# Mixture-of-experts combine weights: spread by DMA through DRAM and applied as the expert activations leave PSUM

## The chip, the cores and the metric

The kernel runs on one core of one Trainium2 chip. The metric is the device time of one execution in microseconds (us). The figure to compare with is the median of three executions of the kernel before, 752.63 us (751.90 to 753.79).

## The reference

The input is `x` (64 sequences, 750 steps, 32 features). Three layers follow each other; `D` is 128, there are 92 patches per sequence, 8 heads and 8 experts:

```python
patches = x[:, idx, :].reshape(B, n_patches, 512)      # patch 16, stride 8 -> 92 patches
h = patches @ W.T + b                                   # (64, 92, 128)

q, k, v = split_heads(layernorm(h) @ w_qkv.T)
attn = softmax(q @ k.T * scale)
attn = einsum('bhij,hg->bgij', attn, reattn_w)          # heads mixed
attn = (attn - mean_heads) * rsqrt(var_heads + 1e-5) * ln_g + ln_b
h = h + (attn @ v) @ w_out.T + b_out

xf = layernorm(h)
scores = softmax(xf @ gate_w.T)
topk_w, topk_i = top_k(scores, 2);  topk_w = topk_w / (topk_w.sum(-1) + 1e-20)
combine[t, topk_i[t]] = topk_w[t]                       # (T, 8), two entries of a row not zero
h1 = relu(xf @ w1[e] + b1[e])                           # for each of the 8 experts
y  = sum_e combine[:, e] * (h1 @ w2[e] + b2[e])
out = h + y + relu(xf @ sw1 + sb1) @ sw2 + sb2          # one shared expert beside the 8
```

## The kernel before, in words

The 64 sequences are worked off in 16 groups of four (`SLOTS` = 4); a group's tile is 128 features by 368 columns (four sequences of 92 patches). All engines run one program of **steps** in the same order, the list `STEPS` (lines 52 to 61), once per iteration `G`. A step is a tuple for one sequence of the attention (`dots`, `max`, `exa`, `exb`, `inv`, `mix`, `sq`, `rstd`, `scale`, `av`, `ev`) or a name for a whole group. `BEHIND` and `LAG` say which sequence or group a step works on in iteration `G`, so that in one iteration the attention of group G runs beside the tokens of group G+1 and the experts of group G-2. Iterations 2 to 13 are a loop on the chip; setup, iterations 0 and 1, and the tail (iterations 14 to 17, with three order lists of their own in `ORDERS_END`) are written out. Each engine executes its own part of the list strictly in that order.

The names that matter here:

- `XE`, `XO`, `TK`, `TH`, `NH`, `TX`: load, transpose, tokens and layernorm of group G+1. `Y0` to `Y7` and `V0` to `V3` make the scores' and the values' operands.
- `OP`, `TH2`, `NH2`, `TX2`: attention output, its layernorm, and the transposed `x2T`, of group G-1.
- `RT`, `R2`, `R3` (function `routing`): the gate's logits and an 18-instruction chain on VectorE that ends in `combine` (line 934), the 8 weights of each token, three copies of them 32 columns apart. Each instruction waits for the one ahead of it.
- `CT`: TensorE transposes `combine` into PSUM, ScalarE and VectorE copy it out as `combT` (lines 653, 771, 1032).
- `Z0` to `Z8`: the first layer of expert e (`Z8` is the shared one), three matmuls each by `products` (lines 335 to 337: high by high, high by low, low by high halves in fp32r). ScalarE empties it with relu and the bias b1 into `act1` (line 786).
- `C0` to `C7`: a matmul of a 0/1 matrix `pick` with `combT` spreads the weights of expert e over the 128 partitions in PSUM (line 660), and VectorE multiplies `act1` with it (line 1041).
- `H0` to `H4`: pairs of experts (`H4` the shared one) are split into a high half (ScalarE, line 753) and a low half (`low_units`, line 405), by GpSimd for `H0`, `H2`, `H4` and by VectorE for `H1`, `H3`.
- `YF`: 27 matmuls of the second layer behind one with `b2_all` that adds the weighted b2 (line 663). VectorE empties it with the residual `h2T` (line 1045). `OT` transposes and stores.

All group steps that use TensorE fill one of three PSUM banks (`ps_fill`, `NBANK` = 3) in turn; `wait_free` makes TensorE wait until the engine that empties the bank's previous content is done, which makes the emptying engine's pace TensorE's affair after two further fills:

```python
FILLS = [step for step in STEPS if isinstance(step, str) and step not in NO_FILL]
BANK = {step: n % NBANK for n, step in enumerate(FILLS)}
```

SP issues two DMAs per iteration: at `XO` the load of `xin` for group G+2, at `OT` the store of `ostage`.

## Time and profile before

| | |
|---|---|
| median of three executions | 752.63 us |
| the profiled execution, its own time | 751.87 us |
| its span, first to last instruction | 750.0 us |
| TensorE (PE) matmuls, busy | 693.2 us, 92% |
| TensorE weight loads (PEld), busy | 627.9 us, 84% |
| VectorE (DVE) | 539.5 us, 72% |
| ScalarE (ACT) | 470.0 us, 63% |
| GpSimd (POOL) | 353.0 us, 47% |
| DMA, mean over the span | 16 GB/s |
| mean granted TensorE clock | 0.97 |

The busy times are those of one profiled execution on the slowest (here the only) core. Matmuls overlap: the busy time of one is longer than the distance to the next, so the pace of TensorE is read from the start times of a timeline or from the pieces of the chain of waits, and not from the mean duration. The chain of waits is followed back from the last instruction, at each step to what released it.

### The profile page before, as it was taken

Reading aid. Unit: us, or ns where it says so; the run is one execution under the profiler, and the core shown is the slowest. Engines: PE = TensorE matmul, PEld = TensorE weight load, DVE = VectorE, ACT = ScalarE, POOL = GpSimd, SP = SyncE. Lnnn points to the kernel's source line nnn. Section 1 sums busy time; section 2 is a strip of 40 time slices with the busy share of each in tenths; the row PEclk is TensorE's granted clock in tenths of the full one; section 3 lists DMA queues with packets and bytes.
Section 4 is the critical chain, followed back from the end, with each engine's and each line's share of the span. In section 5 each row is a group of like instructions: output and inputs, shape, how many; then the busy total and the mean of one; then the engine's idle time right before and its main releaser. Section 6 shows DMA issues by size and latency. Waiting matters only on the chain.

```text
span 750.0 us, 16779 instructions
## 1 busy us (share of the span) xinstructions
PE 693.2 (92%) x5302; PEld 627.9 (84%) x5302; DVE 539.5 (72%) x1559; ACT 470.0 (63%) x1494; POOL 353.0 (47%) x435
## 2 busy tenths in 40 slices
PE   2778999999999999999999999999999999998846
PEld 2568889899898989899898989899898989886735
DVE  1755586968777786968777786968777786966544
ACT  1246476685857666685847666685847676675514
POOL 1534336554553536554554536554554536554302
PEclk9899899999999999999999999999999999998968
DMA  4200000000000000000000000000000000000000
GB/s 99 80 22 1 22 2 22 12 16 8 8 19 10 20 10 20 10 16 8 7 19 10 20 10 20 10 18 7 8 18 10 20 10 2 11 1 11 1 10 11
DMA packets 17058, 12.04 MB, mean 16 GB/s; under 512 B 924, under 2 KB 16776, under 8 KB 17032
## 3 DMA queue, kind: packets, MB, share of 16 engines
q1 hardware_dynamic: 17032, 11.71, 5.7%
q8 instruction: 14, 0.23, 0.1%
q14 instruction: 12, 0.10, 0.0%
HBM read 8.70 MB, written 3.01 MB: 16 GB/s over the span
## 4 chain that ended last, share of the span: by engine, by line
PE 82%; DVE 10%; issue 3%; ACT 2%; DMA 1%; POOL 1%; DVEq 0%; ACTq 0%; POOLq 0%
PE ps_fill L335 16%; PE ps_fill L337 13%; PE ps_fill L336 13%; PE ps_dots L540 11%; PE ps_mix L552 11%; PE ps_fill L495 7%; PE ps_av L560 5%; PE ps_fill L660 3%; DMA xin<-in_x 1%; DVE key L928 1%; DVE top L930 1%; DVE combine L934 1%; DVE yT L798 1%; ACT ex L697 1%; DVE aT L962 1%
## 5 line engine op out<-in xcount | busy, mean ns | idle before, releaser
L1091 POOL TENSOR_TENSOR sum<-sq 92x384 f32<-92x384 f32 x64 | 64.2, 1003 | 203.3 <-ACT sq L705 203.3
L697 ACT ACTIVATE ex<-ps_dots,negmax 128x92 f32<-128x92 f32 x384 | 123.8, 342 | 38.2 <-DVE negmax L943 38.2
L540 PE MATMUL ps_dots<-xT,yT 128*128 128x96 f32 x768 | 96.7, 276 | 7.8 <-ACT ex L697 4.4
L540 PEld LDWEIGHTS ps_dots<-xT,yT 128*128 128x128 f32 x768 | 91.7, 192 | 11.5 <-issue 11.3
L552 PE MATMUL ps_mix<-mixk,probs 128*92 128x128 f32 x768 | 98.5, 280 | 2.1 <-DVE aT L964 1.2
L1085 POOL TENSOR_TENSOR probs<-ex,rinv 128x552 f32<-128x552 f32 x64 | 71.1, 1111 | 52.2 <-DVE rinv L949 52.2
L552 PEld LDWEIGHTS ps_mix<-mixk,probs 128*92 128x92 f32 x768 | 91.0, 165 | 3.4 <-issue 1.6
L1041 DVE TENSOR_TENSOR act<-ps_fill,act 128x368 f32<-128x368 f32 x128 | 64.5, 534 | 40.7 <-PE ps_fill L660 40.3
L786 ACT ACTIVATE act<-ps_fill,vecT 128x368 f32<-128x368 f32 x144 | 76.6, 567 | 27.3 <-PE ps_fill L337 27.1
L405 POOL TENSOR_TENSOR act_split_lo<-act,act_split_hi 128x736 fp32r<-128x736 f32 (+1 forms) x48 | 81.1, 1703 | 25.2 <-ACT act_split_hi L753 24.1
L697 ACT ACTIVATION_READ_ACCUMULATOR ex<-ps_dots,negmax 128x1 f32 x384 | 81.3, 212 | 0.0
L962 DVE TENSOR_TENSOR aT<-ps_mix,arstd 92x360 f32<-92x360 f32 x128 | 61.6, 522 | 5.4 <-ACT arstd L715 4.7
L560 PE MATMUL ps_av<-aT,v_sb 92*64 92x96 f32 x1024 | 57.7, 256 | 3.8 <-DVE aT L964 2.3
L705 ACT ACTIVATE sq<-ps_mix 92x768 f32<-92x768 f32 x64 | 52.3, 817 | 10.8 <-PE ps_mix L552 10.6
L753 ACT ACTIVATE act_split_hi<-act 128x736 fp32r<-128x736 f32 (+1 forms) x80 | 57.1, 753 | 0.9 <-DVE act L1041 0.8
L560 PEld LDWEIGHTS ps_av<-aT,v_sb 92*64 92x64 f32 x1024 | 45.5, 139 | 13.7 <-issue 11.1
L335 PE MATMUL ps_fill<-x2T_hi,w_split_hi 128*128 128x368 f32 x144 | 51.6, 358 | 0.7 <-DVE combT L1035 0.7
L405 DVE TENSOR_TENSOR act_split_lo<-act,act_split_hi 128x736 fp32r<-128x736 f32 x32 | 47.9, 1527 | 5.9 <-ACT act_split_hi L753 5.7
L711 ACT ACTIVATE lnvar<-sumsq,eps 92x96 f32<-92x96 f32 x64 | 24.0, 375 | 41.9 <-POOL sumsq L1098 41.9
L335 PE MATMUL ps_fill<-xT_split_hi,A_hi 128*128 128x368 f32 x128 | 47.7, 372 | 1.9 <-DVE yT L798 1.6
L943 DVE TENSOR_REDUCE negmax<-ps_dots 128x6 f32<-128x552 f32 x64 | 46.3, 723 | 3.3 <-PE ps_dots L540 3.1
L335 PE MATMUL ps_fill<-act_split_hi,w_split_hi 128*128 128x368 f32 x144 | 48.5, 337 | 0.0
(170 smaller groups left out, 1804.1 us busy)
## 6 DMA issues: line engine op xcount, KB each, us to landing
xin<-in_x SPq DMA_DIRECT2D x16, 372.0 KB
out<-ostage SPq DMA_DIRECT2D x16, 184.0 KB
act<-in_L_ffn_w SPq DMA_DIRECT2D x2, 512.0 KB, 4.3
qkv<-in_L_attn_w_qkv SPq DMA_DIRECT2D x1, 768.0 KB, 9.2
ex<-in_L_tok_W SPq DMA_DIRECT2D x1, 256.0 KB
ex<-in_L_attn_w_out SPq DMA_DIRECT2D x1, 256.0 KB
mixw<-in_L_attn_reattn_w SPq DMA_DIRECT2D x8, 0.5 KB
act<-in_L_ffn_sw SPq DMA_DIRECT2D x2, 64.0 KB, 4.4
```

Of the source, the lines that this page charges most:

```text
L335: nc.tensor.matmul(out, s_hi, m_hi, start=start, stop=False)
L336: nc.tensor.matmul(out, s_hi, m_lo, start=False, stop=False)
L337: return nc.tensor.matmul(out, s_lo, m_hi, start=False, stop=stop)
L405: eng.tensor_tensor(lo, act1[:, two, :], hi.bitcast(F32), ALU.subtract).then_inc(done, 1)
L540: last = pe.matmul(ps_dots[:, c // HALF, o:o + NS], yT[:, 2 * s + c // HALF, c % HALF, :, :].rearrange("p h i -> p (h i)"), xT[:, N * s:N ...
L552: last = pe.matmul(ps_mix[0:N, c // HALF, o:o + 128], probs[:, (s - 1) % 2, c, :], mixk[:, :, :].rearrange("p g i -> p (g i)"), start=True ...
L560: last = pe.matmul(ps_av[o:o + DH, NS * (g // 2):NS * (g // 2) + NS], v_sb[:, (s - 2) % SLOTS, DH * g:DH * g + DH], aT[:, s % 2, N * g:N * ...
L697: last = act.activation(ex[:, s % 2, c, :], ps_dots[:, c // HALF, o:o + N], ACT.Exp, bias=negmax[:, c:c + 1], accum_out=sums[:, s % 2, c:c ...
L786: ins = act.activation(act1[:, e, :], ps[:, 0:W], ACT.Relu, bias=vecT[:, e:e + 1])
L962: dve.tensor_tensor(dst, mixed[:, a, :, :, 0:row], scale[:, a, :, 0:row].unsqueeze(2).broadcast_to([N, HALF, HEADS, row]), ALU.mult)
L1041: ins = dve.tensor_tensor(act1[:, e, :], ps[:, 0:W], act1[:, e, :], ALU.mult)
L1085: pool.tensor_tensor(probs[:, s % 2, :, :], ex[:, s % 2, :, :], rinv[:, s % 2, :].unsqueeze(2).broadcast_to([128, CHUNKS, N]), ALU.mult).t ...
```

## The change

- The steps `C0` to `C7`, the matrix `pick` and their matmuls are gone. In place of them SP stores the weights `combine` to a small DRAM tensor at step `R3` (92 x 32 numbers), waits for that, and loads them back with a partition step of 0, so that `spread` holds all 2944 weights of the group in each of the 128 partitions (1472 KB written).
- VectorE empties `Z0` to `Z7` with one instruction, max(x, -b1) times the weight, which is the weighted relu(x + b1) less b1 times the weight. ScalarE keeps only `Z8`. The missing b1 term goes through w2 once, in setup (`pD`), and is added to the rows of b2.
- All five low halves are made by GpSimd.
- `CT` runs one iteration later, since `YF` alone uses `combT` now. A step `hold` on GpSimd copies `h2T` for `YF`, which now runs behind the next group's `OP`.
- `STEPS` and the orders of the tail are new throughout. Three banks remain.

The diff, cut to its core:

```diff
-UNITS_BY_POOL = ("H0", "H2", "H4")
+EXPERTS = tuple(f"Z{e}" for e in range(E))
 UNITS = ("H0", "H1", "H2", "H3", "H4")
...
-    ("dots", 0), "Z0", ("max", 0), "Z1", "Z2", "Z3", "Z4", "C0", ("mix", 0), ("exa", 0), ("sq", 0), "C1", "C2",
+    ("dots", 0), ("max", 0), ("mix", 0), "Z5", "Z6", ("sq", 0), ("av", 0), "Z4", ("exa", 0), "Z3", ("exb", 0),
...
@@ queue of SP
+                if step == "R3":
+                    g = G + LAG[step]
+                    sp.wait_ge(route, N_ROUTE * (g + 1))
+                    sp.dma_start(weights_dram.rearrange("n s e -> n (s e)"), combine[0:N, :, 0:E])\
+                      .then_inc(weights_stored, 16)
+                    sp.wait_ge(weights_stored, 16 * g + 16)
+                    sp.dma_start(spread[:, :, :, :].rearrange("p n s e -> p (n s e)"),
+                                 bass.AP(tensor=weights_dram.tensor, offset=0, ap=[[0, 128], [1, N * SLOTS * E]]))\
+                      .then_inc(weights_spread, 16)
@@ TensorE
+                elif step == "pD":
+                    pe.wait_ge(b1_diag_ready, 1)
+                    pe.wait_ge(experts_loaded, 64)
+                    for e in range(E):
+                        last = pe.matmul(ps[:, 0:128], b1_diag[:, e, :], w2_sb[:, e, :], start=(e == 0),
+                                         stop=(e == E - 1))
-                elif step[0] == "C":
-
-                    pe.matmul(ps[:, 0:W], pick[:, int(step[1]), :], combT[:, :], start=True, stop=True)\
-                      .then_inc(done, 1)
@@ ScalarE
-                elif step[0] == "Z":
-                    e = int(step[1])
...
-                    ins = act.activation(act1[:, e, :], ps[:, 0:W], ACT.Relu, bias=vecT[:, e:e + 1])
+                elif step == f"Z{E}":
+                    at_least(act, units_ready, len(UNITS) * g)
                     wait_filled(act, step, G)
+                    act.activation(act1[:, E, :], ps[:, 0:W], ACT.Relu, bias=vecT[:, E:E + 1])\
+                       .then_inc(emptied[BANK[step]], 1)
@@ VectorE
-                if step[0] == "H" and step not in UNITS_BY_POOL:
-                    low_units(dve, step, G)
-                elif step[0] == "C":
+                elif step in EXPERTS:
+
                     e = int(step[1])
+                    if step == [other for other in order(G) if other in EXPERTS][0]:
+                        dve.wait_ge(weights_spread, 16 * g + 16)
+                        at_least(dve, units_ready, len(UNITS) * g)
                     wait_filled(dve, step, G)
-                    wait_emptied(dve, f"Z{e}", G)
-                    ins = dve.tensor_tensor(act1[:, e, :], ps[:, 0:W], act1[:, e, :], ALU.mult)
-                    ins.then_inc(emptied[BANK[step]], 1)
+                    dve.scalar_tensor_tensor(out=act1[:, e, :].rearrange("p (s n) -> p s n", n=N),
+                                             in0=ps[:, 0:W].rearrange("p (s n) -> p s n", n=N),
+                                             scalar=b1_neg[:, e:e + 1],
+                                             in1=spread[:, :, :, e].rearrange("p n s -> p s n"),
+                                             op0=ALU.max, op1=ALU.mult).then_inc(emptied[BANK[step]], 1)
@@ GpSimd
-                if step in UNITS_BY_POOL:
+                if step in UNITS:
                     low_units(pool, step, G)
+                if step == "hold":
+                    g = G + LAG[step]
+                    wait_emptied(pool, "OP", G)
+                    if present("YF", G):
+                        wait_emptied(pool, "YF", G)
+                    pool.tensor_tensor(still[:, :], ones[:, :], ones[:, :], ALU.mult)
+                    pool.tensor_copy(h2T_held[:, :, :], h2T[:, :, :]).then_inc(held, 1)
```

How the order moves at three places. First VectorE from the instruction that ends `R3` (it writes `combine`) over the end of one iteration (the branch) to the first instructions on the experts in the next, before:

```order
L934 TENSOR_TENSOR combine<-key,top 92x4x3x8
...
L798 COPY v_sb<-ps_fill 92x512
L949 RECIPROCAL rinv<-sums 128x6
L1035 TENSOR_TENSOR combT<-ps_fill,combT 8x368
L982 TENSOR_TENSOR oT_lo<-ps_av,oT_hi 128x4x92
...
L424 COMPARE_AND_BRANCH
L943 TENSOR_REDUCE negmax<-ps_dots 128x6
L1041 TENSOR_TENSOR act<-ps_fill,act 128x368 x3
```

and now (L1090 is the new instruction on the experts, L1098 empties `YF`):

```order
L982 TENSOR_TENSOR combine<-key,top 92x4x3x8
...
L1098 SCALAR_TENSOR_TENSOR fT<-ps_fill,vecT,h2T_held 128x368
...
L1030 TENSOR_TENSOR oT_lo<-ps_av,oT_hi 128x4x92
L1037 TENSOR_REDUCE xsum<-xT 128x4
...
L833 COPY v_sb<-ps_fill 92x512
L1010 TENSOR_TENSOR aT<-ps_mix,arstd 92x3x8x15 x2
...
L453 COMPARE_AND_BRANCH
L991 TENSOR_REDUCE negmax<-ps_dots 128x6
L1090 SCALAR_TENSOR_TENSOR act<-ps_fill,b_neg,spread 128x368 x4
```

`R3` has moved ahead of `YF` and of all eight `Y` steps, and the experts are no longer behind `CT` but behind the DMA.

TensorE at the same turn of the iteration, before (the first row is `CT`, L540 is `dots`, L335 to L337 a `Z`, L660 a `C`, L552 `mix`, L560 `av`):

```order
L495 MATMUL ps_fill<-ident,combine 128x96 x4
...
L424 COMPARE_AND_BRANCH
L540 MATMUL ps_dots<-xT,yT 128x96 x6
L335 MATMUL ps_fill<-x2T_hi,w_split_hi 128x368
...
L660 MATMUL ps_fill<-combT,pick 128x368
L552 MATMUL ps_mix<-mixk,probs 92x128 x6
L660 MATMUL ps_fill<-combT,pick 128x368 x2
L560 MATMUL ps_av<-aT,v_sb 64x96 x8
```

and now (L533 `OT`, L585 `dots`, L597 `mix`, L365 to L367 the first matmuls of `Z5`, L605 `av`):

```order
L533 MATMUL ps_fill<-ident,fT 92x128 x4
...
L453 COMPARE_AND_BRANCH
L585 MATMUL ps_dots<-xT,yT 128x96 x6
L597 MATMUL ps_mix<-mixk,probs 92x128 x6
L365 MATMUL ps_fill<-x2T_hi,w_split_hi 128x368
...
L605 MATMUL ps_av<-aT,v_sb 64x96 x8
```

`Z5` and `Z6` stand ahead of `av`, `Z4` and `Z3` behind it, and nothing at this turn waits for `combine` any more but the DMA's reader.

SP's queue in the loop, before:

```order
L440 DMA xin<-in_x 93x4x256
L480 ISA
L480 DMA out<-ostage 92x4x128
```

and now:

```order
L469 DMA xin<-in_x 93x4x256
L509 REGISTER_ALU
L510 DMA weights<-combine 368x1x8
L512 ISA
L513 DMA spread<-weights 128x2944
L373 ISA
L518 ISA
L518 DMA out<-ostage 92x4x128
```

Two DMAs with a wait between them stand ahead of the output's store.

## Rows read from the trace of the kernel before

**Rows 1.** Busy time in one stretch of the loop, from the table by stretches:
```profile
core 0: us, PE busy (x) PEld busy (x) DVE busy (x) ACT busy (x) POOL busy (x), PEclk, DMA share, GB/s
305.00:350.00 45.00, 44.38 (x353) 40.35 (x353) 35.70 (x105) 30.10 (x97) 23.27 (x30) 1.00 0.05 13
```

**Rows 2.** Timeline of POOL: one step (`shift`) in two iterations that follow each other:
```profile
297.96 0.49 POOL L1123 COPY hT_old<-hT 128x368 f32<-128x368 f32 x1
340.15 0.49 POOL L1123 COPY hT_old<-hT 128x368 f32<-128x368 f32 x1
```

**Rows 3.** Chain of waits near 300 us (start us, us, what): what steps take on TensorE:
```profile
300.81 1.31 PE ps_mix L552 x12
302.12 0.81 PE ps_av L560 x16
302.93 0.40 PE ps_fill L335
303.33 0.23 PE ps_fill L336
...
304.21 1.34 PE ps_dots L540 x12
...
308.26 0.17 PE ps_fill L336
```

**Rows 4.** Groups of instructions by line (busy us, mean ns, idle before and its releaser):
```profile
L660 PE MATMUL ps_fill<-combT,pick 128*128 128x368 f32 x128 | 42.5, 371 | 0.7 <-DVE act L1041 0.3 <-ACT act L786 0.2
L1041 DVE TENSOR_TENSOR act<-ps_fill,act 128x368 f32<-128x368 f32 x128 | 64.5, 534 | 40.7 <-PE ps_fill L660 40.3
L962 DVE TENSOR_TENSOR aT<-ps_mix,arstd 92x360 f32<-92x360 f32 x128 | 61.6, 522 | 5.4 <-ACT arstd L715 4.7
L405 DVE TENSOR_TENSOR act_split_lo<-act,act_split_hi 128x736 fp32r<-128x736 f32 x32 | 47.9, 1527 | 5.9 <-ACT act_split_hi L753 5.7
L1045 DVE SCALAR_TENSOR_TENSOR fT<-ps_fill,vecT,h2T 128x368 f32<-128x368 f32 x16 | 9.6, 600 | 41.3 <-PE ps_fill L337 41.3
L405 POOL TENSOR_TENSOR act_split_lo<-act,act_split_hi 128x736 fp32r<-128x736 f32 x32 | 57.0, 1782 | 25.0 <-ACT act_split_hi L753 23.8
```

**Rows 5.** Timeline of PE where `CT` and the next `dots` start:
```profile
316.14 0.52 PE L495 MATMUL ps_fill<-ident,combine 96*128 96x96 f32 x4 [0.23 <-DVE bias L1030]
316.97 1.57 PE L540 MATMUL ps_dots<-xT,yT 128*128 128x96 f32 x12 [0.31 <-issue]
```

**Rows 6.** Timeline of DVE through `RT`, `R2` and `R3` of one group:
```profile
307.16 0.19 DVE L798 COPY logit<-ps_fill 92x32 f32<-92x32 f32 x1
...
308.48 0.97 DVE L962 TENSOR_TENSOR aT<-ps_mix,arstd 92x360 f32<-92x360 f32 x2
...
310.82 0.18 DVE L911 SCALAR_TENSOR_TENSOR key<-shift_l,rev 92x32 f32<-92x32 f32 x1
...
312.79 0.19 DVE L923 TENSOR_TENSOR hot<-hot 92x32 f32<-92x32 f32 x1
...
313.59 0.17 DVE L927 TENSOR_REDUCE top<-exl 92x4 f32<-92x32 f32 x1
...
315.42 0.32 DVE L934 TENSOR_TENSOR combine<-key,top 92x96 f32<-92x96 f32 x1
```

**Rows 7.** DMA issues (KB each, us to landing), and SP's timeline of the experts' weights:
```profile
qkv<-in_L_attn_w_qkv SPq DMA_DIRECT2D x1, 768.0 KB, 9.2
...
ident<-const_ident SPq DMA_DIRECT2D x1, 64.0 KB, 1.9
...
17.22 0.42 SPq L469 DMA_DIRECT2D act<-in_L_ffn_w  x1
...
18.31 0.43 SPq L471 DMA_DIRECT2D act<-in_L_ffn_w  x1
```

**Rows 8.** The line of the second of these loads, asked alone:
```profile
DMA to landing us min/median/max: 4.8/4.8/4.8
```

**Rows 9.** Timelines of DVE and of SP in the tail, the last group:
```profile
727.65 0.25 DVE L934 TENSOR_TENSOR combine<-key,top 92x96 f32<-92x96 f32 x1
...
745.89 0.26 SPq L480 DMA_DIRECT2D out<-ostage  x1
```

More of the change, by code:

```diff
@@ L136, in order, with first_hidden, last_expert, layout_banks @@
     return STEPS
+def first_hidden(G):
+    return next((step for step in order(G) if step[0] == "Z"), None)
+def last_expert(G):
+    return [step for step in order(G) if step in EXPERTS][-1]
 SETUP = SETUP_START + [step for step in STEPS if present(step, FIRST) and step not in SETUP_START]
 SETUP[SETUP.index("Y5"):SETUP.index("Y5")] = ["pM"]
-SETUP += ["prepE"]
+SETUP += ["pD", "prepE"]
+def layout_banks():
+    last_use = {bank: -1 for bank in range(NBANK)}
+    chosen = {}
+    for n, step in enumerate(SETUP):
+        if step in BANK:
+            last_use[BANK[step]] = n
+        elif step in LAYOUT and not step.startswith("prep"):
+            chosen[step] = min(last_use, key=last_use.get)
+            last_use[chosen[step]] = n
+    return chosen
+BANK.update(layout_banks())
 TAIL = [(step, G) for G in range(END, LAST) for step in order(G) if present(step, G)]
@@ L403, in low_units @@
             hi, lo = [m[:, two, :] for m in act1_split]
[L404 to L405 removed]
+            eng.tensor_tensor(lo, act1[:, two, :], hi.bitcast(F32), ALU.subtract).then_inc(units_ready, 1)
         def bank(step):
@@ L749, in do @@
                     k = int(step[1])
-                    last = f"C{2 * k + 1}" if k < E // 2 else f"Z{E}"
-                    wait_emptied(act, last, G)
+                    for e in range(2 * k, min(2 * k + 2, E + 1)):
+                        wait_emptied(act, f"Z{e}", G)
+                    if step == [other for other in order(G) if other in UNITS][0]:
+                        at_least(act, units_ready, len(UNITS) * g)
+                        if present("YF", G - 1):
+                            wait_filled(act, "YF", G - 1)
                     two = slice(2 * k, min(2 * k + 2, E + 1))
@@ L854, in prepare @@
                 if step == "prepE":
+                    wait_filled(dve, "pD")
                     low = slice((COPIES - 1) * COPY, (COPIES - 1) * COPY + E)
+                    for r in range(COPIES):
+                        rows = slice(COPY * r, COPY * r + E)
+                        last = dve.tensor_tensor(b2_sb[rows, :], bank("pD")[rows, 0:128], b2_sb[rows, :], ALU.add)
+                    last.then_inc(emptied[BANK["pD"]], 1)
+                    wait_emptied(dve, "pD")
                     for r in range(COPIES):
```

92 lines of the change are left out of this document (50 added, 42 removed), and 17 rows, old and new, of tables (ORDERS_END, STEPS).

## The prediction

> **What bounds the kernel now.** I read first the busy time by stretches, since a total mixes setup, loop and tail. In a stretch of the loop TensorE is busy for 44.4 of 45 us, VectorE for 35.7, ScalarE for 30.1 and GpSimd for 23.3, at the full granted clock [rows 1]. So the loop runs at TensorE's pace, and what counts is what TensorE has to do and what newly makes it wait. One iteration takes 42.2 us (340.15 less 297.96) [rows 2]. Then the chain of waits, for the true price of each step on TensorE, since the busy time of one matmul overlaps the next: `mix` 1.31, `av` 0.81, `dots` 1.34, one product of 368 columns 0.17 (so a `Y` or a `Z` 0.51 and `YF` with its 28 some 4.8), and a `V` 0.40 + 2 x 0.23 = 0.86 [rows 3]. Last the timeline around `CT`: TensorE stands for 0.23 us ahead of it and for 0.31 behind it [rows 5], the only waits for routing in the loop.
>
> **The sum is made against the profiled execution's own 751.87 us**, which is 0.8 us under the median of the three runs; that is added at the end.
>
> **C matmuls removed.** Each group loses 8 matmuls of 368 columns. The groups view gives 371 ns for one [rows 4], but that overlaps; the pace is 0.17 us [rows 3], so 8 x 0.17 = 1.36 us per iteration on the engine that bounds. The steps ran in 16 iterations, of which 14 are before the last two of the tail (those go by another sum, below): 14 x 1.36 = **-19.0 us**.
>
> **Gaps at CT.** `CT` now transposes a `combine` that has been ready for half an iteration. The 0.23 and 0.31 us [rows 5] can go, 0.54 us; the lower bound is 0, if TensorE stands there for something else.
>
> **VectorE.** The 8 multiplications of 534 ns become 8 instructions of the kind that empties `YF` (one PSUM operand, one SBUF operand, a pointer scalar), 600 ns [rows 4]: +0.5 us per iteration. The two low halves of 1527 ns go: -3.1. VectorE thus has about 2.5 us less to do, and was not the bound: 0. ScalarE loses 8 emptyings and gets nothing: 0, by TensorE's cover.
>
> **GpSimd** gets two more low halves of 1782 ns [rows 4] and `hold`, a copy like that of `hT_old`, 0.49 us [rows 2], some 4.1 us in all. That takes it from 23.3 of 45 us [rows 1] to about 27, or 61% of a shorter iteration. Behind each low half stand, on GpSimd's queue, the sums for `sq` and the `probs` for `mix` of some sequence. A sequence has a quarter of an iteration, 10 us, for each of its steps, so a delay of 1.8 us is covered; if that cover is gone, `mix` or `av` waits for up to 1.8 us. I take 0. The wait of VectorE's `OP` for `hold` is for a copy made half an iteration earlier: 0.
>
> **A new stall at Y3.** In the new order VectorE has, from the end of `RT` on TensorE to the end of `R3`: 1.3 (307.16 to 308.48), 2.2 (310.82 to 312.98) and 2.15 (313.59 to 315.74) for the three parts of routing, 0.97 for `scale` between them [rows 6], and 0.53 for the low half of `TX`, priced as the 534 ns row [rows 4]. That is 7.2 us. TensorE meanwhile has `TX` (about 0.4 to 0.5, four transposes like `CT` [rows 5]), `YF` 4.8, `mix` 1.3, `Y0` and `Y5` 1.0: 7.5 us. `Y3` then needs the bank of `YF`, which VectorE empties right behind `R3`, 7.2 + 0.6 = 7.8. TensorE waits for about 0.4 us; bounds 0 and 1. With the gaps at `CT` the two come to -0.14 per iteration, over 12 iterations **-1.7 us**.
>
> **The DMA round trip, the step on which all hangs.** The first expert, `Z5`, now waits for `weights_spread`, at the head of VectorE's queue; behind it stand the emptyings of `Z6` and `Z4` and the attention's `ev` and `scale`. How much time is there? `R3` ends 7.2 us after `RT`, TensorE starts `Y3` at 7.8. From there: six `Y` 3.1, `av` 0.8, two `V` 1.7, `OT` 0.4, `dots` 1.3, `mix` 1.3, `Z5` 0.5, together 9.1, so VectorE wants the weights at 16.9. TensorE itself can still fill `Z6`, do `av` and fill `Z4` (1.8 us) before `Z3` needs the bank of `Z5`; with 0.7 for emptying `Z5` that leaves 1.1 us. So the weights have to land by 18.0, which is **10.8 us after R3**.
>
> How long does it take? The store is 368 pieces of 32 bytes. The nearest row is the smallest load, 64 KB in 1.9 us [rows 7]; the other end is the last output store, from its issue at 745.89 [rows 9] to the end of the span, 4.1. I take 1.9, as these are few bytes. The load writes 1472 KB. The experts' weights, 512 + 64 + 512 KB in three loads, were issued from 17.22 on, and the last was issued at 18.31 and landed 4.8 us later [rows 7, 8], 5.9 us for 1088 KB; by their pace 1472 KB take 8.0. The slow end is `qkv`, 768 KB in 9.2 us behind other loads [rows 7], which gives 17.6. I take 8.0, because a row of `spread` is one long run and nothing else is in flight. With 0.2 for two hand-overs the round trip is **10.1 us**, range 9.5 to 21.9, and 0.7 us under what there is. Cost in the loop: 0, with hardly a margin. The Trainium skill (page "DMA: Bandwidth & Descriptors", section on the anatomy of one DMA) fits 2.0 us plus bytes over 436 GB/s for a DMA issued from GpSimd; by it the load would take 5.5 us and the round trip 7.6, well hidden, though no run here shows a broadcast read. The output's store stands behind both DMAs on SP's queue, and has a whole iteration until `ostage` is written again: 0. The load of `xin` is issued at `XO`, behind the first `Z`, so it meets neither.
>
> **Setup.** `pD` adds 8 matmuls with 128 columns in full fp32; six such are a `mix`, 1.31 us, so 1.7. VectorE's part changes by less than a microsecond. TensorE has gaps in setup, so the bounds are 0 and 1.7; I take **+1**.
>
> **Tail.** Here the round trip lies open. Before, from the end of `combine` at 727.90 to the issue of the last store at 745.89, 18.0 us pass [rows 9]. Now: round trip 10.1, `Z0` and `Z1` emptied 1.2, high half 0.8, then four low halves in a row on GpSimd, 7.1 [rows 4], the last six matmuls 1.0, `YF` emptied 0.6, `OT` and its emptying 1.6, in all 22.4, with some hand-overs 23: **+5**. In the iteration before, five low halves on one engine cost some 1 to 2 us more, but `OP` is no longer between `YF` and `TH2` and gives 2.0 back: 0.
>
> **Sum:** -19.0 - 1.7 + 1 + 5 = -14.7, thus 737.2, and 738 against the median. A measurement of this kernel tells about 0.3%, 2.3 us, from no change.
>
> **The rivals.**
>
> *The round trip is longer than its cover (slower).* The place is VectorE's wait at the first `Z` of each iteration. It decides from 10.8 us, and eats the whole gain of 14.7 at 10.8 + 14.7/14 = 11.9 us. For it: 128 partitions and 16 DMA engines read the same 11.8 KB, which no row shows; the store is in small pieces; and the slow end is 21.9. At 14 us each iteration loses 3.2, 14 times 45, and the tail 4 more: 786 us. At 21.9 it would be over 890. Against it: the loads of the experts' weights. Chance 0.22.
>
> *The weights are read slowly from SBUF (no gain).* In the new instruction `spread` is read with a step of 32 numbers, 128 bytes. The nearest row writes `aT` with a step of 15 numbers, and takes 522 ns for 360 elements against 534 for 368 without steps [rows 4], so no penalty shows, but that is a write. If a read took twice the 534 ns, each expert's emptying would take some 1.1 us against 0.5 for the next fill; the Zs come in pairs, and four pairs an iteration with 0.4 us of wait each are 1.6, more than the 1.36 gained: about 754 us. The Trainium skill (page "SBUF — State Buffer", in the section on the DMA port swizzle) says that accesses which cross 16-byte lines pay a penalty, which speaks for this rival. Chance 0.10.
>
> *The new order stalls elsewhere.* A `mix` or `av` that comes 1 us late once per iteration, behind a low half on GpSimd, takes 12 us back: 750. Chance 0.08.
>
> *More than the sum goes.* All small gaps between steps vanish, a further 0.8 us per iteration: 728. Chance 0.06.
>
> *That the change does not do what it says* is out: TensorE's list has no C matmul.
>
> **How the numbers follow.** The forecast, between 730 and 748 by the bounds of the stall at `Y3` (-5 to +7), of setup and of the tail, has 0.54. With the last rival, most of the third, and a part of the DMA rival between 10.8 and 11.9 us, faster by over 0.3% has 0.64; the same 0.08; slower 0.28, from the DMA's 0.20 and parts of the second and third. The range reaches from 724 to 782, where the round trip is 13.7 us; 0.05 is left out below and some 0.15 above.
>
> **What would show it.** Right: the loop's period is near 40.7 us, TensorE stays at 98% of it, the load of `spread` lands within 8 us of its issue, and the first `Z` is emptied without idle time put down to a DMA. The new instruction takes 600 ns; well over 900 would be the second rival. In the tail 23 us from `combine` to the last store's issue. Wrong: VectorE idle ahead of its first expert line, released by a DMA, once per iteration, and TensorE idle 1 us later; or `mix` waiting for GpSimd's `probs`.

## The result, and the profile after

The changed kernel takes **785.71 us** (median of 4, 783.9 to 787.42) against 753.21 for the kernel before in the same comparison (median of 4, 751.9 to 754.99): a ratio of 1.044, 95% interval 1.0409 to 1.0471. It is slower by 32.5 us. 738 was forecast, and the range ended at 782. The profiled execution took 787.42 us, its span is 785.6, its mean granted clock 0.94.

The head of the page, with the slices of the span:

```profile
span 785.6 us, 16622 instructions
## 1 busy us (share of the span) xinstructions
PE 681.7 (87%) x5190; PEld 619.1 (79%) x5190; DVE 541.2 (69%) x1531; ACT 412.9 (53%) x1366; POOL 406.2 (52%) x500
## 2 busy tenths in 40 slices
PE   1687869999999999999999999999999998685735
...
PEclk9679979999999999999999999999999999785967
```

In the middle every slice of TensorE is a 9. What is wrong stands at the ends: in the last six slices it falls to 6, 8, 5, 7, 3, 5, and the granted clock to 7, 8, 5, 9, 6, 7. The time of an execution is best cut where one step recurs. I use the low half of `TX2` on VectorE, once per group (its 3rd start, its 14th, and the end of the span), in these traces:

| kernel | to the 3rd | 11 iterations | period | from the 14th to the end | span |
|---|---|---|---|---|---|
| before | 178.9 | 463.4 | 42.13 | 107.7 | 750.0 |
| after | 187.8 | 455.0 | 41.36 | 142.8 | 785.6 |
| e1_flat_read | 184.0 | 441.3 | 40.12 | 134.8 | 760.1 |
| e2_new_tail | 186.0 | 453.9 | 41.26 | 111.6 | 751.4 |
| e3_new_tail_flat_read | 182.1 | 441.3 | 40.12 | 110.3 | 733.7 |
| e7_no_b1_fold | 179.5 | 452.9 | 41.18 | 112.6 | 745.0 |
| e8_pM_late | 184.5 | 453.3 | 41.21 | 111.2 | 749.0 |
| e9_low_halves_back | 183.8 | 453.6 | 41.24 | 112.0 | 749.4 |
| e11_setup_order | 183.0 | 453.2 | 41.20 | 111.1 | 747.2 |
| e10_all_mended | 179.5 | 439.6 | 39.96 | 112.0 | 731.0 |
| e12_eight_matmuls_more | 178.4 | 451.5 | 41.04 | 114.4 | 744.3 |

The 35.6 us between the spans of before and after are thus +9.0 at the start, **-8.4 in the loop, and +35.1 in the tail**. The first loads do not land at the same time in every execution: VectorE's first instruction starts at 13.6 us before, at 16.1 after, and between 12.9 and 14.7 in the other traces of the table. Differences of 2 us in the first column therefore say little, and 2.5 of the +9.0 may be the loads.

**The loop.** The stretch that stands in [rows 1], now:

```profile
core 0: us, PE busy (x) PEld busy (x) DVE busy (x) ACT busy (x) POOL busy (x), PEclk, DMA share, GB/s
305.00:350.00 45.00, 43.52 (x359) 40.06 (x359) 35.34 (x112) 28.39 (x100) 27.37 (x33) 1.00 0.14 46
```

TensorE is busy for 43.5 of 45 us, where it was 44.4: it waits more than before, not less. GpSimd is at 27.4, as forecast. The gaps at `CT` [rows 5] are gone, and the table of waits from 190 to 600 us has two others, once per iteration each (engine and line, what released it, total us, times, longest):

```profile
PE ps_mix L597 <- DVE aT L1012: 8.8, 10, 1.1
PE ps_dots L585 <- ACT ex L733: 7.1, 10, 0.7
```

The first, 0.88 us, is the stall that the prediction put at `Y3`, one step earlier: `mix` stands right behind `YF`, and needs the `scale` that VectorE does between the parts of routing. The second was not foreseen. ScalarE's timeline shows how it comes about:

```profile
341.45 0.82 ACT L793 ACTIVATE act_split_hi<-act 128x736 fp32r<-128x736 f32 x1 [0.96 <-DVE act L1090]
342.18 0.32 ACT L733 ACTIVATE ex<-ps_dots,negmax 128x92 f32<-128x92 f32 x1
```

The high half `H1` waits for VectorE to empty `Z2`, and behind it in ScalarE's queue stands `exb`, for which TensorE's `dots` waits.

**The instruction and the round trip.** What the trace says of `spread`:

```profile
L1090 DVE SCALAR_TENSOR_TENSOR act<-ps_fill,b_neg,spread x128: 816/867/907, 124.5 to 774.4; 128x368 f32<-128x368 f32 x128
...
  PE ps_fill L367: 21.9, 30
  DMA spread<-weights: 7.7, 2
```

867 ns instead of 600. VectorE waits for the DMA only twice, for 1.0 us at 166 us, in the first iterations of the loop, and for 6.7 us in the last group, where the prediction has the round trip open. From 190 to 600 us it never does. One round trip, first SP's rows, then the first expert of that group on VectorE:

```profile
320.52 0.70 SPq L510 DMA_DIRECT2D weights<-combine  x1
323.33 0.35 SPq L513 DMA_DIRECT2D spread<-weights  x1
```

```profile
330.98 1.64 DVE L1090 SCALAR_TENSOR_TENSOR act<-ps_fill,b_neg,spread 128x368 f32<-128x368 f32 x2 [0.68 <-PE ps_fill L367]
```

The store takes 2.8 us until the load is issued, the load 6.2 (median): 9.1 us from the end of `R3`, landed at 329.5, and the first expert comes at 331.0, released by TensorE and not by the DMA.

**The tail**, cut at the last three starts of the low half of `TX2`. After, then before:

```profile
643.00:704.00 61.00, 49.24 (x325) 44.42 (x324) 31.49 (x83) 25.98 (x86) 27.15 (x34) 0.86 0.09 29
704.00:751.00 47.00, 29.64 (x174) 25.05 (x174) 20.82 (x62) 13.37 (x34) 15.94 (x17) 0.74 0.13 41
751.00:785.00 34.00, 17.58 (x75) 15.55 (x75) 11.87 (x30) 5.54 (x9) 8.06 (x5) 0.70 0.15 50
```

```profile
642.00:682.00 40.00, 39.04 (x307) 34.80 (x305) 29.77 (x84) 27.07 (x90) 20.81 (x27) 1.00 0.02 6
682.00:721.00 39.00, 28.46 (x182) 24.53 (x182) 21.37 (x64) 17.41 (x44) 12.64 (x14) 0.84 0.04 11
721.00:750.00 29.00, 17.58 (x83) 14.90 (x83) 12.43 (x32) 9.69 (x18) 4.88 (x3) 0.74 0.03 7
```

The exact lengths are 60.8, 47.3 and 34.7 us against 40.1, 38.7 and 29.0: +20.7, +8.6, +5.7. The first of them was free of waits before (39 of 40 us busy, full clock). TensorE's largest waits there, with the durations that follow them:

```profile
664.23 1.85 PE L585 MATMUL ps_dots<-xT,yT 128*128 128x96 f32 x12 [1.77 <-ACT ex L733]
671.74 2.52 PE L597 MATMUL ps_mix<-mixk,probs 128*92 128x128 f32 x12 [2.48 <-POOL probs L1139]
...
686.84 0.67 PE L365 MATMUL ps_fill<-oT_hi,woT_split_hi 128*128 128x368 f32 x1 [3.36 <-DVE oT_lo L1030]
```

A `mix` of 1.5 us takes 2.5 here, a matmul of 0.33 us takes 0.67. The granted clock in two of these stretches:

```profile
666.50:668.40 1.90, 1.90 (x9) 1.82 (x9) 0.17 (x1) 1.24 (x3) 0.00 (x0) 0.50 0.00 0
686.80:692.50 5.70, 5.66 (x18) 5.66 (x19) 2.12 (x8) 0.90 (x5) 1.54 (x2) 0.50 0.00 0
```

So behind these pauses TensorE ran at the lower of its two clocks (1.2 GHz), and the pauses cost more than their length. In the first part all waits of TensorE add up to 10.9 us; a mean clock of 0.86 over 61 us is, by an estimate from that row, another 8.5 us. Together they make 19.4 of the 20.7 us.

The second of these waits is the one that the prediction named as a sign of being wrong, `mix` waiting for GpSimd's `probs`. No low half stands in its way:

```profile
670.58 1.11 POOL L1139 TENSOR_TENSOR probs<-ex,rinv 128x552 f32<-128x552 f32 x1 [5.25 <-DVE rinv L997]
```

GpSimd sat idle for 5.25 us until VectorE made `rinv` (step `inv`), which the new order puts behind `CT`, `Z0` and `Z1` in VectorE's queue.

### The profile page after: what moved, and what is told of

It reads as the page before. It is cut to its first block, busy times and chain, and to the rows that moved or that the text cites. A ratio compares the mean times of both kernels' runs of the same rounds, so it can differ in the third digit from the quotient of the medians.

```text
span 785.6 us, 16622 instructions
## 1 busy us (share of the span) xinstructions
PE 681.7 (87%) x5190; PEld 619.1 (79%) x5190; DVE 541.2 (69%) x1531; ACT 412.9 (53%) x1366; POOL 406.2 (52%) x500
## 4 chain that ended last, share of the span: by engine, by line
PE 54%; DVE 24%; issue 7%; ACT 6%; DMA 4%; POOL 3%; SPq 1%; DVEq 0%; ACTq 0%; POOLq 0%
PE ps_fill L365 10%; PE ps_mix L597 9%; PE ps_fill L367 9%; PE ps_fill L366 9%; PE ps_dots L585 8%; DVE act L1090 5%; PE ps_av L605 4%; PE ps_fill L533 4%; DVE aT L1010 3%; ACT ex L733 2%; DMA spread<-weights 2%; DVE hot L960 2%; ACT act_split_hi L793 1%; DVE negmax L991 1%; DMA gate_nat<-in_L_ffn_gate_w 1%
## 5 line engine op out<-in xcount | busy, mean ns | idle before, releaser
L434 POOL TENSOR_TENSOR act_split_lo<-act,act_split_hi 128x736 fp32r<-128x736 f32 (+1 forms) x80 | 127.3, 1600 | 35.9 <-ACT act_split_hi L793 35.7
L1090 DVE SCALAR_TENSOR_TENSOR act<-ps_fill,b_neg,spread 128x368 f32<-128x368 f32 x128 | 107.1, 867 | 29.9 <-PE ps_fill L367 21.9
L597 PE MATMUL ps_mix<-mixk,probs 128*92 128x128 f32 x768 | 102.6, 286 | 25.2 <-DVE aT L1012 21.9
L597 PEld LDWEIGHTS ps_mix<-mixk,probs 128*92 128x92 f32 x768 | 91.3, 168 | 31.4 <-issue 22.7
L585 PE MATMUL ps_dots<-xT,yT 128*128 128x96 f32 x768 | 98.7, 279 | 15.2 <-ACT ex L733 14.5
L585 PEld LDWEIGHTS ps_dots<-xT,yT 128*128 128x128 f32 x768 | 91.5, 193 | 22.1 <-ACT ex L733 12.3
L733 ACT ACTIVATION_READ_ACCUMULATOR ex<-ps_dots,negmax 128x1 f32 x384 | 79.5, 207 | 0.0
L793 ACT ACTIVATE act_split_hi<-act 128x736 fp32r<-128x736 f32 (+1 forms) x80 | 59.1, 765 | 35.5 <-DVE act L1090 35.5
L724 ACT ACTIVATE yT<-ps_fill 128x384 f32<-128x384 f32 x64 | 31.5, 492 | 78.7 <-PE ps_fill L367 78.4
L365 PE MATMUL ps_fill<-x2T_hi,w_split_hi 128*128 128x368 f32 x144 | 56.7, 393 | 11.9 <-DVE act L1090 11.1
L1010 DVE TENSOR_TENSOR aT<-ps_mix,arstd 92x360 f32<-92x360 f32 x128 | 61.6, 522 | 7.8 <-ACT arstd L751 7.7
L605 PE MATMUL ps_av<-aT,v_sb 92*64 92x96 f32 x1024 | 57.8, 256 | 4.4 <-DVE aT L1012 3.5
L605 PEld LDWEIGHTS ps_av<-aT,v_sb 92*64 92x64 f32 x1024 | 46.0, 139 | 13.8 <-issue 10.9
L366 PE MATMUL ps_fill<-x2T_lo,w_split_hi 128*128 128x368 f32 x144 | 50.0, 348 | 0.0
L367 PE MATMUL ps_fill<-x2T_hi,w_split_lo 128*128 128x368 f32 x144 | 50.0, 347 | 0.0
L365 PE MATMUL ps_fill<-xT_split_hi,A_hi 128*128 128x368 f32 x128 | 46.2, 361 | 4.2 <-DVE M L882 1.7
L365 PE MATMUL ps_fill<-act_split_hi,w_split_hi 128*128 128x368 f32 x144 | 48.3, 335 | 0.4 <-POOL act_split_lo L434 0.4
## 6 DMA issues: line engine op xcount, KB each, us to landing
out<-ostage SPq DMA_DIRECT2D x16, 184.0 KB
weights<-combine SPq DMA_DIRECT2D x16, 11.5 KB
```

What stands on the lines that cost most here:

```text
L365: nc.tensor.matmul(out, s_hi, m_hi, start=start, stop=False)
L366: nc.tensor.matmul(out, s_hi, m_lo, start=False, stop=False)
L367: return nc.tensor.matmul(out, s_lo, m_hi, start=False, stop=stop)
L434: eng.tensor_tensor(lo, act1[:, two, :], hi.bitcast(F32), ALU.subtract).then_inc(units_ready, 1)
L585: last = pe.matmul(ps_dots[:, c // HALF, o:o + NS], yT[:, 2 * s + c // HALF, c % HALF, :, :].rearrange("p h i -> p (h i)"), xT[:, N * s:N ...
L597: last = pe.matmul(ps_mix[0:N, c // HALF, o:o + 128], probs[:, (s - 1) % 2, c, :], mixk[:, :, :].rearrange("p g i -> p (g i)"), start=True ...
```

## The experiments

**Theory T** after this reading: the loop does nearly what was forecast; the loss is in the orders that the change writes for the last iterations (`ORDERS_END`), with some in setup. **Rival S**: the slow expert instruction sets everything, in the loop and in the tail. Each experiment was compared with runs of the kernel before on its own chip, whose medians were 752.2 to 752.8 us throughout.

### e1_flat_read: the slow read away

```diff
-    in1=spread[:, :, :, e].rearrange("p n s -> p s n"),
+    in1=spread[:, :, :, :].rearrange("p n s e -> p (n s e)")[:, W * e:W * e + W]
+        .rearrange("p (s n) -> p s n", n=N),
```

> The changed kernel, but VectorE's instruction on expert e reads 368 neighbouring numbers of spread (from 368 e on) in place of every 32nd word; these are the wrong weights, the work and its waits are the same. Theory T (the loss sits in the orders of the last iterations, whose waits are exposed): the instruction falls from 867 to about 600 ns, which gives the loop at most 0.5 us per iteration and the tail some 2 us per iteration, 775 to 781 us. Rival S (the slow read of the weights is the cause): the loop gains another 1 us or more per iteration and the tail comes back too, 755 us or less.

763.56 us (761.91 to 764.65), ratio 1.0145 (1.0093 to 1.0196), 22 us less than after.

```profile
L1090 DVE SCALAR_TENSOR_TENSOR act<-ps_fill,b_neg,spread x128: 554/592/603, 123.0 to 748.9; 128x368 f32<-128x368 f32 x128
```

With neighbouring numbers the same instruction takes 592 ns, what the prediction had priced. The period falls by 1.2 us and `dots` no longer waits for `ex`. The time lies between the two expectations: the slow read is worth 22 us by the medians, more than T gave it and less than all, and the tail is still 27 us longer than before's.

### e2_new_tail: another order for the last iterations

```diff
-ORDERS_END = [[
-    ("dots", 0), ("max", 0), ("mix", 0), ("exa", 0), ("sq", 0), ("exb", 0), ("av", 0), ("rstd", 0), ("dots", 1),
...
+ORDERS_END = [STEPS, [
+    ("mix", 0), "Z8", "CT", ("sq", 0), ("av", 0), "Z0", ("ev", 0), "Z1", ("rstd", 0), ("scale", 0), "Z6", "Z2",
+    ("av", 1), "H4", ("ev", 1), "H0", "OP", "Z3", "TH2", "Z4", "Z5", "NH2", "H1", "Z7", "TX2", "RT", "H2", "R2", "R3",
+    "H3", "YF", "hold", "OT",
+], [
```

> The changed kernel with other orders for two iterations of the tail only: iteration 15 runs the loop's own order (STEPS), iteration 16 puts the Z steps of group 14 under the attention's last chain and under the layernorm of group 15, and YF behind R3. Theory T: iteration 15 falls from 61 to about 41 us and iteration 16 from 47 to about 37, so 30 us less, 755 us. Rival S: the emptying at 867 ns paces these iterations in any order, so less than 10 us are won, over 775 us.

755.58 us (753.24 to 757.74), ratio 1.0046 (1.0019 to 1.0073): **30 us less than after from the order of two iterations alone**, with the instruction still at 866 ns. The three parts of the tail are 39.5, 35.6 and 36.5 us long. The first two have lost 33.0 us, the third is 1.8 us longer.

### e3_new_tail_flat_read: both

> Both edits together (wrong weights again). Theory T: the gain of the new tail plus a few us for the flat read, 745 to 752 us. Rival S: about as e1, since the flat read would already have brought most of it back.

735.75 us (734.95 to 736.27), ratio 0.977 (0.9721 to 0.982). The edits of e1 and e2 add up: -22 and -30 give -50, which is 9 us more than theory T expected here at best. The time is 2 us under the prediction's 738, but by misses that cancel: the period is 40.12 us where the sum has 40.6, the third group still starts 3.2 us later than before, and the tail has an order that the prediction did not price.

### e4_load_twice: a longer round trip

```diff
+    sp.wait_ge(weights_spread, 32 * g + 16)
+    sp.dma_start(spread[:, :, :, :].rearrange("p n s e -> p (n s e)"), ...)
```

> The changed kernel, with the load of spread made twice, the second behind the first's landing; VectorE waits for the second. The round trip grows from about 9.1 to 15.3 us. My step in the prediction (10.8 us of cover from R3 to the first expert): each loop iteration gets 4 to 4.5 us longer, about 45.7 us, and each of the last three iterations some 6: 850 to 860 us. Rival (the cover is larger than worked out): under 2 us per iteration, under 820 us.

877.17 us (873.31 to 883.9), ratio 1.1678 (1.1604 to 1.1753). The period is 47.8 us, 6.4 more, and the time missed the expectation on the high side. The waits from 190 to 600 us, and the granted clock in half an iteration with the wait and in the half behind it:

```profile
DVE act L1094 <- DMA spread<-weights: 45.6, 8, 5.8
PE ps_fill L365 <- DVE act L1094: 31.3, 8, 4.0
```

```profile
305.00:330.00 25.00, 20.44 (x151) 18.68 (x152) 15.47 (x31) 12.87 (x43) 10.99 (x14) 0.86 0.32 120
330.00:353.00 23.00, 22.24 (x176) 20.66 (x176) 17.38 (x64) 12.35 (x42) 14.24 (x19) 1.00 0.12 36
```

A round trip longer by 6.0 us (second load issued at 308.49, the first at 302.47) makes TensorE wait 3.9 us: 2.1 us of cover were unused, so the cover is about 9.1 + 2.1 = 11.2 us, where 10.8 had been worked out. The iteration gets longer by 6.4 us and not by 3.9. The granted clock is lower around the wait: 0.86 over 25 us is, by an estimate, at most 3.5 us more, enough for the rest. Whether the wait also costs something by moving other steps was not measured apart.

This trace also says what does not set the two costly iterations of the tail. Its last three parts take 61.6, 47.3 and 41.3 us, against 60.8, 47.3 and 34.7: with a round trip 6.0 us longer the first grows by 0.8 us, the second not at all, and only the last by 6.7. The expectation of some 6 us for each was wrong, and the DMA is out as the cause of the +20.7 and +8.6.

### e5_step_32_bytes and e6_flat_layout: can the read be made fast?

```diff
-    sp.dma_start(weights_dram.rearrange("n s e -> n (s e)"), combine[0:N, :, 0:E])
+    sp.dma_start(bass.AP(tensor=weights_dram.tensor, offset=0, ap=[[E, N], [N * E, SLOTS], [1, E]]),
+                 combine[0:N, :, 0:E])                                               # e5
+    for s in range(SLOTS):                                                           # e6
+        sp.dma_start(bass.AP(tensor=weights_dram.tensor, offset=N * s, ap=[[1, N], [W, E]]),
+                     combine[0:N, s, 0:E])
```

VectorE's index into `spread` is changed to fit in both.

> The tail's new order stays (755.58 us with the weights read at a step of 128 bytes, 735.75 with neighbouring numbers). The store writes the weights in another order, so that one expert's 368 weights lie 32 bytes apart in each row of spread instead of 128. Theory L (a read at any step over 16 bytes pays the same): the instruction stays at 866 ns, the time at 753 to 758. Theory B (only a large step pays, by banks or lines of 64 bytes or more): the instruction falls to between 600 and 700 ns and the time to 737 to 745. The store is still 368 pieces of 32 bytes, so the round trip should stay at 9.1 us.

> A true layout with one expert's 368 weights side by side: the store is four DMAs (one per sequence) of 736 pieces of 4 bytes each, all else as in e2_new_tail. The instruction must come to 592 ns, as in e1_flat_read. If the store in small pieces is as fast as before (theory: a DMA costs by its fixed part), the round trip stays under 10 us and the time is 736 to 739. If the pieces cost (rival), with 2944 pieces against 368 and four issues in a row, the round trip is 11 to 14 us, over its cover of some 11, VectorE waits for the DMA once per iteration, and the time is 745 to 790.

e5: 754.51 us (752.6 to 757.95), ratio 1.0043 (1.0025 to 1.0061), no different from e2, as theory L has it. e6: 998.7 us (997.16 to 1001.03), ratio 1.3288 (1.3254 to 1.3322), far beyond both expectations. The instruction in e5 and in e6:

```profile
L1082 DVE SCALAR_TENSOR_TENSOR act<-ps_fill,b_neg,spread x128: 831/895/975, 120.6 to 740.9; 128x368 f32<-128x368 f32 x128
```

```profile
L1084 DVE SCALAR_TENSOR_TENSOR act<-ps_fill,b_neg,spread x128: 554/593/602, 134.2 to 984.2; 128x368 f32<-128x368 f32 x128
```

895 ns (median) at a step of 32 bytes, 867 at 128, 593 for neighbours. The Trainium skill (page "SBUF — State Buffer", in the section on the DMA port swizzle) says that accesses which cross 16-byte lines are penalized, without a figure. The three rows agree with it, as both steps are over 16 bytes and pay about the same; a step under 16 bytes was not tried. And e6's stores, one group:

```profile
338.27 9.66 SPq L503 DMA_DIRECT2D weights<-combine  x4
355.67 0.34 SPq L507 DMA_DIRECT2D spread<-weights  x1
```

2944 pieces of 4 bytes in four DMAs take 17.4 us until the load can be issued; 368 pieces of 32 bytes in one took 2.8. Neighbouring numbers alone were worth 20 us (e3 against e2), and e6 is 243 us slower than e2. It has both smaller pieces and four DMAs in place of one; the two were not separated.

### e7, e8 and e11: the setup

e7 leaves out the fold of b1 (seven matmuls of `pD`, the three additions to `b2_sb`). e8 and e11 only move steps:

```diff
-SETUP[SETUP.index("Y5"):SETUP.index("Y5")] = ["pM"]
+SETUP[SETUP.index("BS"):SETUP.index("BS")] = ["pM"]                                  # e8
+SETUP[SETUP.index("BS"):SETUP.index("BS")] = ["pM", "prepX", "pD", "prepE"]          # e11, no others elsewhere
```

> As e2_new_tail, but the fold of b1 into the bias rows is left out (seven of the eight matmuls of pD and the three additions to b2_sb), so the output lacks b1 times w2. Theory: the fold lies on the path of setup ahead of the first row maximum, matmuls about 1.8 us and additions 0.9; the start of the third group comes 2 to 3 us earlier than 185.98 and the time is 752.5 to 754. Rival: it is hidden behind other work in setup; no change, 755 to 756.

> As e2_new_tail, but in setup pM (the product of the weights for the output) comes ahead of BS, its first user, and not ahead of Y5, which in the new order of steps has moved to the front of the Ys. Theory: the Ys of the first group no longer wait for VectorE's copy of M and its matmuls, TensorE idles less between 30 and 45 us and the time falls by 1 to 3 us, to 752.5 to 754.5. Rival: setup is bounded by VectorE and the loads at that place, so that the same wait appears one step later: 755 to 756, no change.

> As e2_new_tail, but in setup pM, prepX, pD and prepE come ahead of BS. e7 without the fold of b1 was 8.5 us faster, and e8 with pM moved 3.6 us. Theory: both costs are costs of place, since VectorE does the additions of prepE and the five instructions of prepX at a moment when TensorE waits for it; at BS VectorE stands idle for 2 us. Then the first hT_old (52.97 in e2, 50.31 in e8, 48.44 in e7) comes at 47 to 49 and the time is 747 to 750. Rival: what setup adds is work that has to be done somewhere ahead of the first maximum: 751 to 752, as e8.

e7: 747.12 us (746.84 to 748.7), ratio 0.994 (0.9919 to 0.9961). e8: 751.92 (750.28 to 753.16), ratio 0.999 (0.9978 to 1.0003). e11: 748.86 (745.46 to 749.39), ratio 0.9939 (0.9915 to 0.9963). VectorE in e2 at the end of setup, ahead of the first row maximum:

```profile
46.73 0.88 DVE L893 TENSOR_TENSOR b_sb<-ps_fill,b_sb 8x128 f32<-8x128 f32 x3 [1.79 <-PE ps_fill L557]
...
48.67 0.73 DVE L983 TENSOR_REDUCE negmax<-ps_dots 128x6 f32<-128x552 f32 x1
```

The same steps in e11:

```profile
40.49 0.88 DVE L892 TENSOR_TENSOR b_sb<-ps_fill,b_sb 8x128 f32<-8x128 f32 x3 [0.24 <-PE ps_fill L556]
...
44.41 0.73 DVE L982 TENSOR_REDUCE negmax<-ps_dots 128x6 f32<-128x552 f32 x1 [1.16 <-PE ps_dots L576]
```

The fold holds VectorE's queue in e2 for 3.7 us (1.79 waiting for `pD`, then 1.9 from 46.73 on), with the first softmax behind it. Moved ahead of `BS` it starts 6.2 us earlier, and the first row maximum (`negmax`) 4.3 us earlier. By the medians e7 is 8.5 us under e2, e8 3.7 and e11 6.7; the third group's start gives 6.5, 1.5 and 3.0. Part of the gap between the two figures is that e2's profiled execution was 2.3 us under its median. e7 and e8 came out below what was expected of them, e11 within it. So leaving the fold out is worth 6.5 to 8.5 us, where the prediction had 1 for all of setup, and moving steps alone wins 3.0 to 6.7 back. How much of that is the fold's is not shown, since e11 moves `pM` and `prepX` with it.

### e9_low_halves_back: H1 and H3 on VectorE again

```diff
+UNITS_BY_POOL = ("H0", "H2", "H4")
+UNITS_BY_DVE = ("H1", "H3")
...
+    done = units_ready if step in UNITS_BY_POOL else dve_units
```

> As e2_new_tail, but the low halves H1 and H3 are on VectorE again, as in the kernel before. If moving them to GpSimd was free in the loop, as the prediction has it, putting them back costs or gives nothing while VectorE keeps up: with the expert instructions at 866 ns VectorE gets 2 x 1.53 us more, 38.4 of 41.3 us, and every emptying and aT behind H1 comes up to 1.5 us later. Theory V (VectorE is already the engine that TensorE waits for, at mix and dots): the period rises from 41.27 by 0.5 to 2 us, 762 to 780. Rival G (the low halves on GpSimd delay probs and thereby the attention): the period falls, 750 to 754.

752.79 us (750.86 to 755.04), ratio 1.0003 (0.9983 to 1.0023); the period is 41.24 us against 41.26. In this loop, which still has the waits at `mix` and `dots`, it does not matter which engine makes them, though VectorE's busy time rises to 38.2 of 45 us. V falls. G's sign does not show in the period either, though the time lies in its range: of the 2.8 us under e2, 2.2 stand in the first column of the table, where the loads differ from one execution to the next. The row that surprised:

```profile
L430 DVE TENSOR_TENSOR act_split_lo<-act,act_split_hi x32: 872/913/1004, 132.5 to 740.6; 128x736 fp32r<-128x736 f32 x32
```

913 ns here, where the same instruction had a mean of 1527 in the kernel before [rows 4].

### e10_all_mended: a version that beats both

The new tail, the setup of e11, and two moves in the loop, one for each of TensorE's waits:

```diff
-    "XO", ("ev", 1), ("mix", 1), "Z7", "Z2", ("exa", 1), ("sq", 1), "OP", "H1", "Z1", ("exb", 1), "shift",
+    "XO", ("ev", 1), ("mix", 1), "Z7", "Z2", ("exa", 1), ("sq", 1), "OP", "Z1", ("exb", 1), "H1", "shift",
...
-    ("inv", 2), "V2", "RT", "R2", ("rstd", 2), "TX", ("scale", 2), "R3", ...
+    ("inv", 2), "V2", "RT", "R2", ("rstd", 2), ("scale", 2), "TX", "R3", ...
```

> As e11_setup_order, with two more moves in the loop's order: H1 goes behind the second exb, and the second-to-last scale ahead of TX. They are meant for the two stalls of TensorE per iteration that are left (0.72 us ahead of dots for ex, 0.76 ahead of mix for aT). Theory: both are set by what stands ahead on ScalarE and VectorE, so the period falls from 41.27 to between 40.1 and 40.7, and the time to 735 to 742, below both kernels. Rival: the wait comes back one step later (YF, Y0 or TK), period 41.0 to 41.3, 746 to 750.

**731.57 us** (729.77 to 734.04), ratio **0.9717** (0.9691 to 0.9743): 21 us faster than the kernel before, 54 faster than after, with 867 ns per expert instruction. It came out better than its expectation. The loop's stretch, and what is left of TensorE's waits in it:

```profile
305.00:350.00 45.00, 44.38 (x353) 40.85 (x353) 37.17 (x109) 27.10 (x93) 25.70 (x33) 1.00 0.15 47
```

```profile
PE ps_mix L588 <- DVE aT L1003: 2.7, 10, 0.3
```

TensorE is back at 44.4 of 45 us, the wait ahead of `dots` is gone, the one ahead of `mix` is 0.27 us. The two moves gave 1.24 us per iteration (41.20 to 39.96), and 17 us against e11.

### e12_eight_matmuls_more: the price of the largest term

```diff
                 elif step == "CT":
+                    for _ in range(E):
+                        pe.matmul(ps[:, 0:W], b2_all[:, :], combT[:, :], start=True, stop=True)
```

> As e10_all_mended, plus eight matmuls of 368 columns ahead of the transposes of CT, in the form of the C matmuls that the change removed; their result is written over. This prices the largest term of the prediction by itself, in a loop that waits for nothing but TensorE. Theory: 0.17 us each on the pace, 1.36 us per group; the period rises from 39.96 to 41.3 us and the time from 731.6 to 750 to 755 (16 groups, 22 us). Rival: part of them goes into time in which TensorE waits anyway (0.3 us ahead of mix), or the price is the 0.33 us that the groups view gives one (2.6 per group, 773 us); below 0.1 us each, under 745, the term was too high.

747.22 us (746.13 to 749.36), ratio 0.994 (0.9917 to 0.9963), 15.6 us over e10. TensorE's timeline at the place, first e10, then e12:

```profile
321.78 1.50 PE L576 MATMUL ps_dots<-xT,yT 128*128 128x96 f32 x12
323.12 0.49 PE L524 MATMUL ps_fill<-ident,combine 96*128 96x96 f32 x4
```

```profile
324.00 1.50 PE L576 MATMUL ps_dots<-xT,yT 128*128 128x96 f32 x12
325.28 1.57 PE L690 MATMUL ps_fill<-combT,b_all 128*128 128x368 f32 x8
326.70 0.49 PE L524 MATMUL ps_fill<-ident,combine 96*128 96x96 f32 x4
```

From `dots` to the transposes it is 1.34 us in the one and 2.70 in the other: 1.36 on the spot, to the hundredth the prediction's term per iteration. The period rises by only 1.08 (39.96 to 41.04), so later steps give 0.28 back; which ones is open. So one such matmul was worth 0.13 to 0.17 us, the time missed its expectation on the low side by 3 us, and the term of -19.0 was too large by about a fifth at most (14 x 1.08 = 15.1).

## Why the prediction was wrong

The sign was wrong, and most of the chance of "slower" lay on a rival that was not the cause. Cut as in the table, the sum had -2 us up to the third group, -16.5 in the 11 iterations and +3.6 in the tail; measured were +9.0, -8.4 and +35.1. By its own steps:

- **C matmuls, -19.0.** Right in kind and nearly in size: e12 prices them at 15 to 19 us over 14 iterations.
- **Gaps at CT, -0.54 per iteration.** Right: no wait for routing is left in the loop. What its going gave was not measured apart.
- **The stall at Y3, +0.4.** The chain through routing, `scale` and `TX` was the right one. The wait was 0.88 us, and it came at `mix`, the first step behind `YF` that needs any of VectorE's work; I had looked only for the next bank. In e10, with `scale` one place forward, 0.27 is left.
- **VectorE's expert instruction, 600 ns, "0".** Mis-sized: 867. The price was taken from a row with the same operands but without a step in the SBUF read. The second rival had the mechanism, a slow read, and I gave it a tenth, because a *write* with a step showed no penalty [rows 4]. The sentence of the Trainium skill that it cites (page "SBUF — State Buffer", in the section on the DMA port swizzle: each access that crosses to a new line pays a penalty) agrees with the rows of e1 and e5. Its place was wrong: TensorE does not wait at the `Z` pairs but at `dots`, by way of `H1` on ScalarE. Its 754 us left out the +6 of setup and tail; by the prediction's own terms it comes to 760. Worth: 22 us by the medians (e1). Between the two profiled executions it is 25.5 us, 13.7 in the loop, 8.0 in the tail and 3.8 ahead of the third group, where VectorE's first instruction also starts 3.0 us earlier.
- **Low halves and hold on GpSimd, 0.** Right in the loop for the low halves (e9); `hold` was not tested by itself.
- **DMA round trip, 10.1 us against 10.8.** 9.1 against about 11.2: right, and the first rival (0.22) is out. Its parts were off in both directions: the store took 2.8 instead of 1.9, the load 6.2 instead of 8.0. The Trainium skill (page "DMA: Bandwidth & Descriptors", section on the anatomy of one DMA) has a fit for a DMA issued from GpSimd, and the estimate of 5.5 us by it was closer than the row I used, though this DMA was issued from SP. That rival's estimate of 786 us happens to be the measured time, for a reason that does not hold; the coincidence says nothing for it.
- **Setup, +1.** Mis-sized: the third group starts 9.0 us late, of which 2.5 may be the loads. The term counted TensorE's matmuls and left out that `prepE` stands ahead of the first maximum in VectorE's queue and waits there for `pD` (e7, e11), and that the new order puts `pM` ahead of seven of the eight `Y`s, where five stood ahead of it before (e8).
- **Tail, +5: the step that failed.** The last group took what was worked out, 23.7 us from `combine` to the last store's issue (757.80 to 781.52) for 23, and +5.7 in all; in part by luck, since the first expert came 8.8 us behind `combine` where the sum has a round trip of 10.1, and the rest took 14.9 for 12.9. But "in the iteration before ... 0" was written for two iterations whose orders are new from the first line to the last. They cost +20.7 and +8.6. I had read the order of the loop step by step and not theirs. e2 shows that the order is the cause: 30 us come back from it alone, with the read still slow; e4 shows that the DMA is not.

The mis-sized terms are thus 29 us (two iterations of the tail), +9.0 for +1 up to the third group, and 22 for the read. They overlap and cannot be added: of the read's share of the tail 6.9 us lie within the 29. e10, with another tail, another setup and the two waits of the loop moved away in spite of the slow read, takes 731.6, 6 us *below* the forecast; so the sum of the loop was on the cautious side, by an order that the prediction did not describe. By the sum its period should be 42.13 - 1.36 - 0.54 + 0.27 = 40.5; it is 39.96. That half microsecond per iteration is not explained; it is in the direction of the rival "more than the sum goes". It does not lie in idle time that the profile shows: TensorE's busy time per period fell by 1.95 us, from 41.57 to 39.62, and the 8 matmuls are 1.08 to 1.36 of that.

## What to carry to other kernels

Where an order is written out by hand, price each order that the change touches, with as much care for an iteration that runs once as for the loop: here 2 of 18 iterations lost 29 us, more than the loop had to win. For every instruction that gets later or longer, follow each queue it stands in to the first step that TensorE takes from that queue; the wait shows up there and not at the next bank. Before borrowing a duration from another row, compare the access pattern of every operand, reads as well as writes: here one operand's step made 867 ns of 592.
